# One engine's share of the weight groups moved on odd tiles, and all seven first-layer groups split: a one-core recommender kernel

## What is computed

```python
X0 = e                                   # (512, 39, 16), gathered rows
Xi = X0
for W, b in [(W0, b0), (W1, b1), (W2, b2)]:
    Wr = W.reshape(128, 39, Xi.shape[1])
    Xi = einsum('hjk,bjd,bkd->bhd', Wr, X0, Xi) + b[None, :, None]
    res.append(Xi.sum(axis=2))
z = concatenate(res, axis=1)
h = maximum(concatenate([z, dense_ctx], axis=1) @ W_top1 + b_top1, 0)
h = maximum(h @ W_top2 + b_top2, 0)
y = h @ W_top3
```

## Time and profile before

| what | us |
|---|---|
| median of 3 runs | 665.23 (664.14 to 666.54) |
| the profiled execution | 665.45 |
| its span, first to last instruction | 663.6 |
| PE busy | 648.5 (98%) |
| DVE busy | 558.7 (84%) |
| POOL busy (DMA issuing left out) | 468.5 (71%) |
| ACT busy | 440.8 (66%) |

### The profile page before, as it was taken

The page is one execution under the profiler, slowest core; times in us unless marked ns, Lnnn a source line. Parts: engine busy times, 40 slices in busy tenths (PEclk is TensorE's granted clock), DMA queues, the critical chain, the costliest instruction groups (busy, mean ns, idle before and its releaser), DMA issues.

```text
span 663.6 us, 11303 instructions
## 1 busy us (share of the span) xinstructions
PE 648.5 (98%) x3070; PEld 518.3 (78%) x3070; DVE 558.7 (84%) x1558; ACT 440.8 (66%) x1449; POOL 468.5 (71%) x376
## 2 busy tenths in 40 slices
PE   7998999999999999999999999999999999999997
PEld 7785678777788777777778877778778887777877
DVE  4669899999984799999995699999997589999970
ACT  3554667677763777777773677877785477778761
POOL 6888888888873688888875478787876367444540
PEclk8899999999999999999999999999999999999999
DMA  6013474140403004040311301313040300400000
GB/s 216 14 36 107 130 243 128 23 120 8 128 10 114 16 8 128 6 122 16 94 44 45 90 5 46 91 29 108 18 121 15 107 17 8 126 2 5 1 1 1
DMA packets 38357, 42.25 MB, mean 64 GB/s; under 512 B 17824, under 2 KB 22549, under 8 KB 38166
## 3 DMA queue, kind: packets, MB, share of 16 engines
q1 hardware_dynamic: 32661, 40.23, 19.9%
q0 software_dynamic: 5632, 1.31, 2.2%
HBM read 8.84 MB, written 0.00 MB: 13 GB/s over the span
## 4 chain that ended last, share of the span: by engine, by line
PE 92%; DVE 2%; DMA 2%; ACT 1%; issue 1%; POOL 1%; SPq 0%; POOLq 0%; DVEq 0%
PE p_u L804 22%; PE p_u L806 21%; PE p_u L805 21%; PE p_x L779 6%; PE p_tower L827 5%; PE p_g L818 5%; PE p_x L776 2%; PE p_x L774 2%; PE p_x L773 2%; PE p_tower L854 1%; DMA g_all<-w_in 1%; PE p_x L744 1%; DVE parts L636 1%; DVE z L595 1%; PE p_x L756 1%
## 5 line engine op out<-in xcount | busy, mean ns | idle before, releaser
L457 ACT ACTIVATE prod<-p_u,x0t 128x128 f32<-128x128 f32 x1024 | 290.4, 376 | 101.5 <-PE p_u L806 101.4
L636 DVE SCALAR_TENSOR_TENSOR parts<-p_u,x0t,parts 128x128 f32<-128x128 f32 x1024 | 283.4, 341 | 41.3 <-PE p_u L806 41.2
L804 PE MATMUL p_u<-w1h,x1h 128*128 128x512 f32 (+1 forms) x640 | 288.4, 451 | 1.0 <-ACT x1h L438 1.0
L806 PE MATMUL p_u<-w1h,x1l 128*128 128x512 f32 (+1 forms) x640 | 250.2, 391 | 0.0
L805 PE MATMUL p_u<-w1l,x1h 128*128 128x512 f32 (+1 forms) x640 | 250.1, 391 | 0.0
L335 POOL DMA_INDIRECT emb<-table_in,idx_all x176 | 207.9, 1181 | 49.9 <-issue 47.5
L354 POOL TENSOR_TENSOR parts<-parts,prod 128x512 f32<-128x512 f32 x128 | 176.2, 1377 | 51.7 <-ACT prod L457 38.3
L804 PEld LDWEIGHTS p_u<-w1h,x1h 128*128 128x128 f32 x640 | 120.9, 189 | 37.9 <-issue 8.6
L805 PEld LDWEIGHTS p_u<-w1l,x1h 128*128 128x128 f32 x640 | 121.5, 190 | 35.6 <-issue 10.8
L806 PEld LDWEIGHTS p_u<-w1h,x1l 128*128 128x128 f32 x640 | 120.7, 189 | 26.1
L349 POOL TENSOR_TENSOR parts<-prod 128x512 f32<-128x512 f32 x64 | 83.3, 1301 | 73.0 <-ACT prod L457 72.2
(11 more groups left out here) (86 smaller groups left out, 388.2 us busy)
## 6 DMA issues: line engine op xcount, KB each, us to landing
fac_b<-xx SPq DMA_DIRECT2D x90, 234.0 KB
fac_a<-xx SPq DMA_DIRECT2D x45, 78.0 KB
emb<-table_in,idx_all POOLq DMA_INDIRECT x176, 3.2
g_all<-w_in SPq DMA_DIRECT2D x3, 832.0 KB, 6.2
w<-w_in SPq DMA_DIRECT2D x1, 2496.0 KB, 9.2
xx<-xx SPq DMA_DIRECT2D x30, 78.0 KB
fac_b<-xx SPq DMA_DIRECT2D x15, 156.0 KB
bd<-x0t SPq DMA_DIRECT2D x120, 10.0 KB
```

The source lines that it names most:

```text
L457: last = nc.scalar.activation(dst[:, i * H:(i + 1) * H], u[:, i * H:(i + 1) * H], ACT.Copy, scale=x0t[:, par, t, j:j + 1])
L636: nc.vector.scalar_tensor_tensor(out=chain[i][:, p], in0=u[:, i * H:(i + 1) * H], scalar=x0t[:, par, t, j:j + 1], in1=add, op0=ALU.mult, o ...
L804: nc.tensor.matmul(u, xh, wh, start=True, stop=False)
L806: nc.tensor.matmul(u, xl, wh, start=False, stop=True).then_inc(u_full, 1)
```

## The change

On every odd tile from 5 to 61 (29 tiles, called wide here) ACT takes six quads, 0, 2, 4, 5, 7 and 9, and DVE four, 1, 3, 6 and 8. GpSimd has five `prod` to sum there, so four additions. Even tiles, tiles 1 and 3 and tile 63 stay at five and five. All waits that counted by tile count by tables now. `prod` grows from eight to nine buffers. `SPLIT` names all seven groups. The slot tables are not touched, so a new low half sits three slots before PE's use of it, as the others do. The core of the diff; the waits on `a_scaled`, `chained` and `summed` in the parts left out change in the same way, from tile times a constant to `A_DONE`, `V_DONE` and `SUMS_DONE`:

```diff
-SPLIT = (0, 2, 4, 6)
+SPLIT = tuple(range(GROUPS))
...
-CHAIN_TILE = 20
-A_TILE = 5
-SUM_TILE = 3
+WIDE = [T % 2 == 1 and TILES < T < TILES_BLOCK * BLOCKS - 1 for T in range(TILES_BLOCK * BLOCKS)]
+A_QUADS = [(0, 2, 4, 5, 7, 9) if wide else (0, 2, 4, 6, 8) for wide in WIDE]
+V_QUADS = [(1, 3, 6, 8) if wide else (1, 3, 5, 7, 9) for wide in WIDE]
+A_DONE = [sum(map(len, A_QUADS[:T])) for T in range(len(WIDE) + 1)]
+V_DONE = [4 * sum(map(len, V_QUADS[:T])) for T in range(len(WIDE) + 1)]
+SUMS = [len(A_QUADS[T]) - 2 for T in range(len(WIDE))]
+SUMS_DONE = [sum(SUMS[:T]) for T in range(len(WIDE) + 1)]
+PRODS = [4, 5]
...
-        prod = sb("prod", [128, 2, 4, 4 * H])
+        prod = sb("prod", [128, sum(PRODS), 4 * H])
...
-                    for i in (2, 3):
-                        pool.wait_ge(a_scaled, A_TILE * T + 2 + i)
-                        pool.wait_ge(summed, SUM_TILE * T + i - 1)
+                    for i in range(2, SUMS[T] + 1):
+                        pool.wait_ge(a_scaled, A_DONE[T] + 2 + i)
+                        pool.wait_ge(summed, SUMS_DONE[T] + i - 1)
...
-                        if q % 2 == 0:
+                        if q in A_QUADS[T]:
                             scale_quad(T, tt, q)
...
-                k = q // 2
+                k = V_QUADS[T].index(q)
                 dve.wait_ge(u_full, QUADS * T + q + 1)
...
-                        if q % 2 == 1:
+                        if q in V_QUADS[T]:
                             chain_quad(T, tt, q)
...
-                if q0 % 2 == 0:
-                    pe.wait_ge(a_scaled, A_TILE * T0 + q0 // 2 + 1)
+                if q0 in A_QUADS[T0]:
+                    pe.wait_ge(a_scaled, A_DONE[T0] + A_QUADS[T0].index(q0) + 1)
                 else:
-                    pe.wait_ge(chained, CHAIN_TILE * T0 + 4 * (q0 // 2 + 1))
+                    pe.wait_ge(chained, V_DONE[T0] + 4 * (V_QUADS[T0].index(q0) + 1))
```

More of the change, by code:

```diff
@@ L339, in pairs @@
             def pairs(p, i):
-                return prod[:, p, i, :].rearrange("p (a i h) -> p a i h", a=2, i=2)
+                return prod[:, p * PRODS[0] + i, :].rearrange("p (a i h) -> p a i h", a=2, i=2)
             def body(n, has_prev, has_next):
@@ L345, in body @@
                     p, m, t = tt % 2, tt // TILES, tt % TILES
-                    pool.wait_ge(a_scaled, A_TILE * T + 3)
+                    pool.wait_ge(a_scaled, A_DONE[T] + 3)
                     need(pool, x2_made, T - 1)
@@ L408, in evac_x0t @@
                     act.wait_ge(f_bd_in, 16 * TILE_B)
-                need(act, chained, CHAIN_TILE * TILES * (M - 1))
-                need(act, a_scaled, A_TILE * TILES * (M - 1))
+                need(act, chained, V_DONE[TILES * (M - 1)])
+                need(act, a_scaled, A_DONE[TILES * (M - 1)])
                 need(act, bd_in[par], 16 * TILE_B * pair)
@@ L449, in scale_quad @@
                 if q == 0:
-                    need(act, chained, CHAIN_TILE * (T - 2) + 4)
+                    if T > 1:
+                        act.wait_ge(chained, V_DONE[T - 2] + 4)
                     dst = start[:, p].rearrange("p a h -> p (a h)")
                 else:
-                    need(act, summed, SUM_TILE * (T - 2) + 3)
-                    dst = prod[:, p, q // 2 - 1, :]
+                    if T > 1:
+                        act.wait_ge(summed, SUMS_DONE[T - 1])
+                    dst = prod[:, p * PRODS[0] + A_QUADS[T].index(q) - 1, :]
                 u = p_u[(QUADS * tt + q) % RING]
@@ L623, in chain_quad @@
                 p, par, t = tt % 2, (tt // TILES) % 2, tt % TILES
-                k = q // 2
+                k = V_QUADS[T].index(q)
                 dve.wait_ge(u_full, QUADS * T + q + 1)
                 if k == 0:
-                    dve.wait_ge(a_scaled, A_TILE * T + 1)
+                    dve.wait_ge(a_scaled, A_DONE[T] + 1)
                     need(dve, x2_made, T - 1)
@@ L634, in chain_quad @@
                         add = chain[i][:, p]
-                        dve.wait_ge(chained, CHAIN_TILE * T + 4 * (k - 1) + i + 1)
+                        dve.wait_ge(chained, V_DONE[T] + 4 * (k - 1) + i + 1)
                     nc.vector.scalar_tensor_tensor(
@@ L640, in fold_x2 @@
             def fold_x2(T, p):
-                dve.wait_ge(chained, CHAIN_TILE * (T + 1))
-                dve.wait_ge(summed, SUM_TILE * (T + 1))
+                dve.wait_ge(chained, V_DONE[T + 1])
+                dve.wait_ge(summed, SUMS_DONE[T + 1])
                 need(dve, g_full, T - 1)
```

## The result

The changed kernel takes 696.02 us (median of 4 runs, 695.30 to 697.11) against 665.88 us before (4 runs): a ratio of 1.0448, 95% interval 1.0414 to 1.0482. That is 30 us slower, where 26 were forecast, inside the range and above the forecast value of 691. The profiled execution has a span of 694.3 us against 663.6.

The account below looks back on a forecast made before the run. PE, busy 98%, was taken as the bound. Steady macros 11 x (1.7 + 1.0) = 29.7, tower macros 2.6 and PE work -6.3 gave +26 us: 691 us, range 670 to 708.

Parts of the forecast that it names:

- PE's saving: Three more groups split in each of 14 macros save PE 0.15 us each, 6.3 us; steady macro 35.22 to 34.77 us.
- Groups 1, 3, 4 and 6 by their chains: PE waits for low halves late behind DVE's ordered instructions: 0.35, 0.52, 0.2 and 0.2 us a steady macro.
- The 0.1 for each restart: PE's record after each stop lasts 0.50 in place of 0.40 us; 0.1 us added for each of four stops.
- The holds: DVE instructions with two SBUF operands wait out POOL's additions: 1.0 us a steady macro, 0.4 of it in group 1.
- The setting-out: DVE's and POOL's work laid out for one macro, giving 2.0 us of holding on top of PE's waits.
- the halving: Half of the 2.0 us, 1.0, was taken because POOL shifts against PE from macro to macro.
- Tower macros: Macros 4, 8 and 12: only group 1 comes before PE slows at slot 15; 0.45 plus 0.4 us each.
- The Trainium skill's rule: Two-SBUF-input DVE and SBUF-reading GpSimd instructions exclude each other for a whole instruction; it speaks for 704 us.
- the upper end: All of the 2.0 us in steady macros and 1.25 us in each tower macro: +38 us, 704 us.
- Low halves in time: Rival: PE gets its low halves in time and the 6.3 us are gained, 659 us; chance 0.10.
- POOL sets the pace: Rival: POOL at 35.5 us a macro exceeds PE's 34.77, the fold waits for sums, 665 us; chance 0.06.
- Stops without holds: Rival: PE's waits come but POOL's additions fall between as before, +13.8 us, 679 us; chance 0.24.

Follow-up runs that it names:

- Low halves early with small additions: The changed kernel with every low half one slot earlier, group 1's two, and GpSimd's additions cut to 16 of 512 columns; one run, steady macros 35.2 us.
- five-split kernel: Kernel before with group 3 split too (0, 2, 3, 4, 6), five and five quads on every tile; ratio 0.999, macros 5 to 7 35.0 us.
- the change with small additions: The changed kernel with GpSimd's additions cut to 16 of 512 columns, the other sums left out; ratio 1.012 against before, macros 5 to 7 36.2 us.

## Why the prediction was right, and where it was off

- **PE's saving** (6.3 us, 34.77 us a macro): right within 0.05 us a macro. Low halves early with small additions takes 35.19 with 0.27 and 0.1 of stop in it, so 34.8; and one group more in the five-split kernel takes 0.2 us off.
- **Groups 1, 3, 4 and 6 by their chains** (0.35, 0.52, 0.2, 0.2 us): with the holds removed they measured 0.31, 0.53, 0.21 and 0.02 (macro 1 apart, where group 1 has 1.04). Three agree within 0.05; group 6's wasn't there. Groups 0, 2 and 5 had no stop, as worked out. The 0.1 for each restart is in every record behind a stop (0.50).
- **The holds** (1.0 us a steady macro, half of the 2.0 set out): this is the mis-sized term. They measured 38.2 - 36.2 = 2.0 in macro 6. The setting-out had given 0.9 in group 1, where 1.08 was measured, 0.3 in group 3 (0.29), 0.1 in group 4 (0.12) and 0.7 in group 6 (0.46). The step that was off is the halving, on the ground that POOL's phase against PE shifts from macro to macro: both engines' work follows PE's quads, and the stops repeat from block to block, in most places within hundredths (group 3's 0.82 in the steady macros from 3 to 13 is 1.10 in macro 7). In group 1 it differs by the place in the block: macros 5, 9, 13 and 14 have stops of 0.7 to 0.8, macro 1 none, and the others 1.2 to 1.4. The forecast for a steady macro was 2.25 us net (2.7 of stops less 0.45). Measured from transpose to transpose it is 2.7 to 3.3 in six macros (2, 3, 6, 7, 10, 11), 2.3 in those three, 2.0 in 14 and 1.4 in 1. Their sum is 28.4 us against 24.8, and with the tower macros (1.0, 0.05 and 1.0, against 0.4 each) that is most of the gap between 691 and 696: it is made by the six macros that have the whole hold. One length in the holds' paragraph, 1.31 us for the first of the two additions, isn't what its subtraction gives: 3.04 - 1.59 = 1.45 is the distance between their starts. The record itself is 1.31 us long, so the 0.55 stands.
- **Tower macros** (0.85 with hold): the stop in group 1 was 1.25 to 1.4 us, the whole hold again; groups 3 to 6 had none, as said. Macro 8 got no longer all the same, since before's own macro 8 (51.0 us) is 0.8 longer than its macros 4 and 12.
- **The Trainium skill's rule** on the port pair (SBUF — State Buffer, "Who interferes with whom") was set at the upper end, 704 us. The exclusion that it states is what the runs show: the holds end 0.54 to 0.56 us behind an addition, and with additions of 16 columns the held time fell from 26.1 to 0.0 us. That ports are behind it, no run here can show. The upper end came out too high because group 6's and the post-tower macros' terms were smaller.
- **Rivals.** *Low halves in time*: it needed group 3's stop to be absent, and without holds that stop is 0.53. *POOL sets the pace*: against it speaks that DVE's folds never wait for the sums in the change (their idle time after 90 us is 0.5 us in all, for DVE's own `parts`), and that with POOL at 15.5 us a macro the change still takes 36.2. *Stops without holds*: it was 679 us, and the kernel that realises it has a ratio of 1.012, some 674 us from 665.9; it isn't what happened, since the holds are there.

**How much of it was luck.** From macro 1's transposes to the end before takes 589.9 us, the change with small additions 599.0 and the change 620.4. So the chains less PE's saving cost 9.2 us, where 13.8 were forecast, and the holds 21.4, where 12.2 were (11 x 1.0 + 3 x 0.4). The two misses point opposite ways: that the time came within 5 us of 691 is in part luck, while the direction and the range rest on terms that were measured.

## What to carry over

On an engine that works in order, an operand's lateness is the longest chain in front of it from the last thing that engine waited for, and not its busy share: the change made DVE lighter per macro and PE waited for it all the same. Where VectorE instructions with two SBUF operands and GpSimd additions share a loop, read from the trace where each begins inside the other before adding either or moving one by a slot; here one more low half of 0.60 us cost 1.9% in one slot and nothing in another. If such a phase pattern repeats in before, set it out whole and don't discount it.

## What the runs showed of the hardware that I had not expected

- An addition's record can begin after that of the VectorE instruction it holds: 305.96 against 305.81, and the latter still ended only at 307.83, 0.56 us behind the addition. So a start earlier by 0.15 us in the records doesn't mean that it went first.
- TensorE's granted clock fell to the lower level for 3.4 us, 0.2 to 1.5 us after a stop of 2.0 us had ended, while PE was busy again, in six places. Three of nine equal stops in the same kernel had no such effect, nor had the stops of up to 1.4 us in the change (clock 1.00 from macro 1 to the end).
- GpSimd's gathers took 1.05 us on average with small additions, where they took 1.18 before. The traces give a hint: in the change, gathers whose records overlap none of DVE's products, low halves or x1l take 1.00 us (1.01 at most), the 101 that do 1.25 on average, and 1.05 with small additions. Which is the cause wasn't isolated.
